# Constants filled inside the encoder program, identity products in TensorE's first waits, and other orders in the last encoder step, the first cross items and the tail

## The reference

```python
# 1: six layers of causal linear attention with MLP, 16 heads of 16, over x flipped along the sequence
for l in range(6):
    a = causal_linear_attn(elu(q) + 1, elu(k) + 1, v) @ Wo[l] + bo[l]
    x = layer_norm(x + a, g1[l], be1[l])
    x = layer_norm(x + gelu(x @ W1[l] + b1[l]) @ W2[l] + b2[l], g2[l], be2[l])
x = layer_norm(x + flip(layer_norm(x)))       # final norm gf, bf, then the residual
# 2: differential cross attention against ctx_1024
attn = softmax(q1 k1 / 4) - gain * softmax(q2 k2 / 4)
x = layer_norm(x + norm_per_head(attn @ v) @ wo.T)
# 3: three cycles of a coupling net
for _ in range(3):
    tf = sigmoid(gelu-net of three layers(out) @ cn_w4 + cn_b4)
    coupling = 0.1 + adaptive_range * (0.7 * gf + 0.3 * tf - 0.5) * 2.0
    out = out + coupling * twist(out)         # twist: (p_r, -p_i, -o_r, o_i)
return layer_norm(x + out)
```

## Time and profile before

| | us |
|---|---|
| median of 3 runs | 1529.33 (1527.33 to 1529.43) |
| profiled execution | 1529.64 |
| its span, first to last instruction | 1527.9 |
| PE busy in the span | 1463.5 |
| DVE, POOL, ACT busy | 1248.2, 1024.9, 984.4 |

### The profile page before, as it was taken

How to read it: one execution, slowest core, us unless ns; L and a number is a source line. 1 busy time by engine, 2 the same in 40 slices (tenths; PEclk the granted TensorE clock), 3 DMA queues, 4 the chain that set the end, 5 groups by cost and what they waited for, 6 DMA issues and landing times. The chain is left out here.

```text
span 1527.9 us, 38603 instructions
## 1 busy us (share of the span) xinstructions
PE 1463.5 (96%) x15935; PEld 1163.1 (76%) x15935; DVE 1248.2 (82%) x2076; ACT 984.4 (64%) x1608; POOL 1024.9 (67%) x970
## 2 busy tenths in 40 slices
PE   6799999999999999999999999999999899999897
PEld 4688888888888888888888888888887566665434
DVE  5888989889898888888888888988784799998546
ACT  4566667666666666667667666666644788887445
POOL 4356667766677566776667766677558599986534
PEclk8899999999999999999999999999999999999999
DMA  5010011110111101210012100110205455443001
GB/s 162 13 60 19 19 26 42 60 24 19 26 46 57 21 19 26 64 42 19 19 26 70 38 17 19 26 43 13 40 9 152 129 165 168 150 154 87 1 0 56
DMA packets 91766, 81.99 MB, mean 54 GB/s; under 512 B 17652, under 2 KB 79816, under 8 KB 91592
## 3 DMA queue, kind: packets, MB, share of 16 engines
q1 hardware_dynamic: 91592, 79.54, 18.3%
HBM read 50.79 MB, written 14.68 MB: 43 GB/s over the span
## 5 line engine op out<-in xcount | busy, mean ns | idle before, releaser
L789 POOL TENSOR_TENSOR e_h_lo<-e_h_f,e_h_hi 128x512 fp32r<-128x512 f32 x192 | 261.7, 1371 | 200.3 <-ACT e_h_hi L581 198.0
L580 ACT ACTIVATE e_h_f<-e_pr,e_h_bias 128x512 f32<-128x512 f32 x192 | 132.0, 688 | 217.9 <-PE e_pr L181 213.3
L900 DVE TENSOR_TENSOR e_am<-e_sc,c_amask 128x1024 f32<-128x1024 f32 x192 | 225.8, 1217 | 51.2 <-PE e_sc L428 51.2
L1900 DVE TENSOR_REDUCE x_mx<-x_psS 128x4 f32<-128x1024 f32 x128 | 154.4, 1210 | 32.1 <-PE x_psS L1484 31.9
L179 PE MATMUL e_tr<-e_W_hi,e_h_hi 128*128 128x256 f32 x576 | 166.1, 288 | 1.1 <-POOL e_h_lo L789 1.1
L179 PE MATMUL e_pr<-e_yT_hi,e_W_hi 128*128 128x512 f32 x384 | 166.8, 434 | 0.3 <-ACT e_h_hi L581 0.3
L180 PE MATMUL e_tr<-e_W_lo,e_h_hi 128*128 128x256 f32 x576 | 163.7, 284 | 0.0
L181 PE MATMUL e_tr<-e_W_hi,e_h_lo 128*128 128x256 f32 x576 | 163.5, 284 | 0.0
L1652 ACT ACTIVATE x_ex<-x_psT 128x1024 f32<-128x1024 f32 x128 | 131.1, 1024 | 43.2 <-PE x_psT L1506 40.5
L180 PE MATMUL e_pr<-e_yT_lo,e_W_hi 128*128 128x512 f32 x384 | 151.6, 395 | 0.0
L181 PE MATMUL e_pr<-e_yT_hi,e_W_lo 128*128 128x512 f32 x384 | 149.8, 390 | 0.0
(11 more groups left out here) (299 smaller groups left out, 4370.2 us busy)
## 6 DMA issues: line engine op xcount, KB each, us to landing
e_raw_m<-in_L_attn_W_dram SPq DMA_DIRECT2D x12, 1024.0 KB, 5.2
x_qs<-query_rows SPq DMA_DIRECT2D x48, 256.0 KB
e_x_raw<-e_x_blocks SPq DMA_DIRECT2D x352, 32.0 KB, 1.9
x_ks<-key_rows SPq DMA_DIRECT2D x48, 128.0 KB, 2.7
query_rows<-x_q_hi SPq DMA_DIRECT2D x16, 256.0 KB, 2.1
query_rows<-x_q_lo SPq DMA_DIRECT2D x16, 256.0 KB, 2.3
x_ctok<-in_ctx_dram SPq DMA_DIRECT2D x8, 256.0 KB, 2.9
x_xo<-in_x_dram SPq DMA_DIRECT2D x8, 256.0 KB, 2.8
```

Source lines behind the costliest of these rows:

```text
L580: act.activation(h_f[:, m % HR, :], ps_pr[m % 2][:, :], ACT.Gelu, bias=h_bias[:, l * FC + m:l * FC + m + 1])
L789: pool.tensor_tensor(h_lo[:, m, :], h_f[:, m % HR, :], h_hi[:, m, :].bitcast(F32), ALU.subtract).then_inc(h_lo_done, 1)
L900: dve.tensor_tensor(am[:, s % 2, c, :, :, :], ps_sc[:, :, c * 2 * P:(c + 1) * 2 * P].rearrange("p r (h n) -> p r h n", n=P), amask[:, :].u ...
L1900: dve.tensor_reduce(mx[:, N % 2, :, 0:HG].rearrange("p i (a h) -> p h a i", a=2)[:, pair], ps_s[pair][:, :, :].rearrange("p a (i j) -> p a ...
```

## The change

GpSimd fills the constants at the head of its encoder program and the separate block is gone; PE waits for the identity alone (semaphore value 2) and multiplies it by itself into free PSUM banks, 11, 8 and 5 times at the start and 8, 14 and 10 times in the step u = 0. The Exp table is asked for at ACT's start. In the last step but one `mlp_up(7)` stands behind the second Wo block and `gelu(7)` behind `attn_hi(1)`. The encoder's last moments and their power move behind the first cross statistics on DVE and POOL, and POOL does `rsqrt(0, 2)` ahead of `keys_lo(1)`. In the tail DVE writes the first tile's couplings and applies half of the last two tiles' norm.

```diff
@@ tensor, step @@
+                def kept_busy(bank, n):
+                    for _ in range(n):
+                        pe.matmul(bank[:, 0:P], ident[:, :], ident[:, :], start=True, stop=True)
+
                 if q < 0:
+                    pe.wait_ge(consts["ready"], consts["unit"])
+                    kept_busy(ps_pr[0], 11)
                     pe.wait_ge(consts["ready"], consts["count"])
                     pe.wait_ge(x0_loaded, 16)
...
+                    kept_busy(ps_pr[0], 8)
                     pe.wait_ge(biases_loaded, 16 * len(BIASES))
...
+                    kept_busy(ps_pr[0], 5)
...
+                if u == 0:
+                    kept_busy(ps_tr[1], 8)
                 if attn:
                     pe.wait_ge(phi_done, 4 * t + 4)
...
+                if u == 0:
+                    kept_busy(ps_tr[1], 14)
                 if attn:
                     pe.wait_ge(ktok_done, t + 1)
...
+                if u == 0:
+                    kept_busy(down_bank(3), 10)
...
                     mlp_up(6)
-                    mlp_up(7)
+                    if following or not attn:
+                        mlp_up(7)
...
+                        elif mlp and s == 2:
+                            mlp_up(7)
                         pe.wait_ge(aT_lo_done, 2 * t + s // 2 + 1)
@@ scalar, step @@
                 if q < 0:
+                    act.wait_ge(consts["ready"], consts["count"])
+                    act.activation(table[:, :], consts["ident"][:, 0:1], ACT.Exp)
...
-                    gelu(7)
+                    if following or not attn:
+                        gelu(7)
...
                     attn_hi(1)
+                if mlp and attn and not following:
+                    gelu(7)
@@ gpsimd @@
             cross = nxt.gpsimd(pool)
+            consts["fill"](pool)
...
-            rsqrt(2, final)
-
...
-            cross.items({N: last_shifted(s) for s, N in enumerate(LAST_SHIFTED)})
+            cross.items({LAST_MOMENTS: lambda: rsqrt(2, final), **{N: last_shifted(s) for s, N in enumerate(LAST_SHIFTED)}})
@@ vector @@
-            moments(2, final)
...
-            cross.items({N: last_rows(half) for half, N in enumerate(LAST_USED)})
+            cross.items({LAST_MOMENTS: lambda: moments(2, final), **{N: last_rows(half) for half, N in enumerate(LAST_USED)}})
@@ cross stage, gpsimd items @@
             x1_norm(1)
+            rsqrt(0, 2)
             keys_lo(1)
-            rsqrt(0, 2)
@@ feed forward @@
+            k, late = j // 2, j % 2
+            if k < PAIRS:
+                sp.wait_ge(y_done, 2 * j + 2)
+            elif late:
+                sp.wait_ge(norm_step, READY * NT + 2 * (k - PAIRS) + 2)
+            else:
+                sp.wait_ge(y_done, SB * PAIRS + 2 * (k - PAIRS) + 2)
             sp.dma_start(ov[:, 2 * j:2 * j + 2], X[:, 2 * j:2 * j + 2]).then_inc(stored, 16)
...
-                    for i in range(PAIRS):
-                        shares(stage, i)
+                    shares(stage, 1)
             for k in range(NT):
-                apply(k)
+                apply(k, SB if k < PAIRS else SB // 2)
...
-            for b in range(2 if stage < HALVES - 1 else 0):
+            for b in range(2 if stage < HALVES - 1 or i == 0 else 0):
...
+        def apply(k):
+            dve.wait_ge(rs_done, 2 * k + 2)
+            for s in range(SB // 2, SB):
+                dve.tensor_scalar(X[:, k * SB + s, :], half_bank(k, s), rs[:, k, s:s + 1], shift[:, k, s:s + 1],
+                                  ALU.mult, ALU.add).then_inc(norm_step, 1)
...
             norm(3)
+            apply(2)
+            apply(3)
```

More of the change, by code:

```diff
@@ L163, in encoder @@
     LNS = {1: 2, 2: 3}
+    LAST_MOMENTS = 0
     LAST_NORMED, LAST_SHIFTED, LAST_USED = (9, 10, 17, 25), (11, 12, 20, 28), (29, 37)
@@ L565, in step @@
                 if attn:
-                    act.activation(table[:, :], consts["ident"][:, 0:1], ACT.Exp)
+                    if q >= 0:
+                        act.activation(table[:, :], consts["ident"][:, 0:1], ACT.Exp)
                     for j in range(2 * KC):
@@ L2119, in sync @@
         for j in range(NB // 2):
-            sp.wait_ge(y_done, 2 * j + 2)
+            k, late = j // 2, j % 2
[5 more added lines that the diff above has]
+                sp.wait_ge(y_done, SB * PAIRS + 2 * (k - PAIRS) + 2)
             sp.dma_start(ov[:, 2 * j:2 * j + 2], X[:, 2 * j:2 * j + 2]).then_inc(stored, 16)
@@ L2285, in fourth, with apply @@
             act.activation(th[:, tile(stage, i), :], banks[L4_BANK[i]][:, :], ACT.Tanh, bias=b4h[:, :], scale=0.5).then_inc(a4, 1)
-        def apply(k):
+        def apply(k, rows):
             act.wait_ge(rs_done, 2 * k + 2)
-            for s in range(SB):
+            for s in range(rows):
                 act.activation(X[:, k * SB + s, :], half_bank(k, s), ACT.Identity, bias=shift[:, k, s:s + 1],
@@ L2298, in shares @@
                 act.activation(cp[:, k, cols], th[:, k, cols], ACT.Identity, bias=offset[:, 2 * k + b:2 * k + b + 1],
-                               scale=slope[:, :]).then_inc(cp_done, 1)
+                               scale=slope[:, :]).then_inc(a4, 1)
         def rows_in(k, bank):
@@ L2465, in shares @@
                                   ALU.mult, ALU.add).then_inc(cp_done, 1)
-            dve.wait_ge(cp_done, 2 * n + 2)
+            if stage < HALVES - 1 or i == 0:
+                dve.wait_ge(cp_done, 2 * n + 2)
+            else:
+                dve.wait_ge(a4, PAIRS * HALVES + 2)
             if stage > 0:
@@ L2525, in constants @@
     blockmask = consts["blockmask"][:, :].rearrange("p (h d) -> p h d", d=HX)
-    with nc.Block() as block:
-        @block.gpsimd
-        def _(pool):
-            pool.memset(ident, 0.0).then_inc(filled, 1)
-            for table in (amask, headmask, consts["blockmask"][:, :]):
-                pool.memset(table, 1.0).then_inc(filled, 1)
-            pool.memset(consts["half"][:, :], -0.5).then_inc(ready, 1)
-            pool.wait_ge(filled, 4)
-            pool.affine_select(ident, ident, [[-1, P]], ALU.not_equal, 1.0, base=0, channel_multiplier=1).then_inc(ready, 1)
-            pool.affine_select(amask, amask, [[-1, P]], ALU.is_ge, 0.0, base=0, channel_multiplier=1).then_inc(ready, 1)
-            pool.affine_select(headmask, headmask, [[-DH, HC]], ALU.is_ge, 0.0, base=0, channel_multiplier=1).then_inc(lower, 1)
-            pool.affine_select(blockmask, blockmask, [[-DH, HC], [0, HX]], ALU.is_ge, 0.0, base=0, channel_multiplier=1).then_inc(lower, 1)
-            pool.wait_ge(lower, 2)
-            pool.affine_select(headmask, headmask, [[DH, HC]], ALU.is_ge, 0.0, base=DH - 1, channel_multiplier=-1).then_inc(ready, 1)
-            pool.affine_select(blockmask, blockmask, [[DH, HC], [0, HX]], ALU.is_ge, 0.0, base=DH - 1, channel_multiplier=-1).then_inc(ready, 1)
@@ L2546, in constants, with fill @@
-    consts["ready"], consts["count"] = ready, 5
+    def fill(pool):
+        pool.memset(ident, 0.0).then_inc(filled, 1)
+        for table in (amask, headmask, consts["blockmask"][:, :]):
+            pool.memset(table, 1.0).then_inc(filled, 1)
+        pool.memset(consts["half"][:, :], -0.5).then_inc(ready, 1)
+        pool.wait_ge(filled, 4)
+        pool.affine_select(ident, ident, [[-1, P]], ALU.not_equal, 1.0, base=0, channel_multiplier=1).then_inc(ready, 1)
+        pool.affine_select(amask, amask, [[-1, P]], ALU.is_ge, 0.0, base=0, channel_multiplier=1).then_inc(ready, 1)
+        pool.affine_select(headmask, headmask, [[-DH, HC]], ALU.is_ge, 0.0, base=0, channel_multiplier=1).then_inc(lower, 1)
+        pool.affine_select(blockmask, blockmask, [[-DH, HC], [0, HX]], ALU.is_ge, 0.0, base=0, channel_multiplier=1).then_inc(lower, 1)
+        pool.wait_ge(lower, 2)
+        pool.affine_select(headmask, headmask, [[DH, HC]], ALU.is_ge, 0.0, base=DH - 1, channel_multiplier=-1).then_inc(ready, 1)
+        pool.affine_select(blockmask, blockmask, [[DH, HC], [0, HX]], ALU.is_ge, 0.0, base=DH - 1, channel_multiplier=-1).then_inc(ready, 1)
@@ L2547, in constants @@
+    consts["ready"], consts["count"], consts["unit"], consts["fill"] = ready, 5, 2, fill
     return consts
```

## The result

The changed kernel takes 1520.11 us (median of 4 runs, 1519.69 to 1521.38) against 1528.84 (4 runs, 1527.33 to 1529.43): the ratio is 0.9949, 95% interval 0.9937 to 0.9961. Its profiled execution took 1520.41 us with a span of 1518.7, 9.2 us less than the span of before. Forecast were 6.4 us less.

What follows compares the result with a forecast made beforehand. It took PE, busy 96% of the span, as the bound. Terms -3.0 - 1.0 - 0.6 - 1.3 - 0.5 = -6.4 from the profiled 1529.64 gave 1523.2 us, range 1519.5 to 1527.5.

Steps and rivals of the forecast that it cites:

- The block: At the start: without the constants block SP issues its first load at about 0.79, 2.72 us sooner; `X` there at 5.0.
- The start's products: At the start: products take back nearly all the block gives, clock rises at 6.6, queries at 11.15; start's term -3.0 us.
- 27.8 to 37.3: 0: Low-clock stretch from 27.8 to 37.3 us, without products: should fall to 1.2 GHz again, so 0 gained.
- The rival that the clock stays up there: Rival: the clock also stays up from 27.8 to 37.3, some 2.5 us more, 1520.7 us; chance 0.12.
- u = 0: 1.0: Step u = 0: products 0.2 us late, but full clock saves 1.2; term -1.0 us, between 0 and -1.3.
- Last step but one: 0.6: Last encoder step but one: moved `mlp_up(7)` fills PE's 1.83 us wait, POOL limits the gain; -0.6 us, 0 to -1.4.
- First items: 1.3: First cross items: reordering removes PE waits of 0.64 and 0.71 us; term -1.3 us, between 0 and -2.0.
- Tail: 0.5: Kernel end: ACT and DVE share the norm, so the last transfer issues sooner; -0.5 us, between -0.2 and -0.9.
- Late engines: Rival at the start: the other engines don't leave the first meeting at 0.79; 1524.1 us, chance 0.09.
- Constants held back by DVE's clearing: Rival at the start: the identity comes 2.1 us later, start's term -0.9; 1525.3 us, chance 0.08.
- Late rise and nothing at the borders: Rival: late clock rise at the start, POOL's queue and SP's order take back the steps' gain; 1527.3 us, chance 0.14.
- Products that don't raise the clock: Rival at the start and u = 0: identity products leave the clock at 1.2 GHz; +6.0 us, 1535.6 us, chance 0.05.

Runs made afterwards that it cites:

- e1: The changed kernel without its 24 identity products at the start; 1520.96 us.
- e6: The kernel before with only the constants moved into GpSimd's encoder program and the early Exp table; 1526.31 us, ratio 0.9981.
- b2: The changed kernel with 6, 3 and 0 identity products at the start, and 5, 8 and 10 added in the first step's waits; 1516.52 us.
- e5: The changed kernel run again, unchanged; 1520.36 us.

## Why the prediction was right in range and short in size

- **The block** (SP at 0.79, `X` at 5.0). Right: 0.79 in every trace, `X` at 4.56 and 4.96 where nothing stood ahead of it (e1, e6), instead of 7.73, and e6 alone gives 2.4 us by 22.67 and 3.1 in the median, against 2.72.
- **The start's products.** The forecast let the clock rise at 6.6, within 5.85 to 7.25; the two traces of the program have 7.9 and 5.2, and gains of 3.09 and 4.41 us, the latter beyond the term's bound of 3.4. "The products take back nearly all that the missing block gives" is right. That the queries began at 11.13, against 11.15, is in part luck: the clock rose 1.3 us later than taken, and the products were shorter (0.44 and 0.22 us against 0.45 and 0.24). What the sum lacked is that the clock without them is as loose: it rose 3.7 us after the first query in e1, 5.4 after it before and 5.8 in e6.
- **27.8 to 37.3: 0.** This term failed, 1.30 us in the first trace. "Should fall to 1.2 GHz again" was right, that it would last as long was not: 10.2 us in six of the ten traces without products in that step, 6.8 in four, with one program on both sides. And what it takes differs less from trace to trace than its length, since a short one followed a late start (3.09 and 1.30) and a long one an early start (4.41 and 0.25). The rival that the clock stays up there did not come: it fell in both traces of the changed kernel. Only b2 and its successors, with products there, kept it up.
- **u = 0: 1.0.** The clock was 1.00 throughout, and from `mlp_up(0)` to the second scores came 1.09 us by the clock against 1.17. The 0.2 us of delay was a gain of 0.2 us. 1.29 in the trace, at the upper bound of 0 to 1.3.
- **Last step but one: 0.6.** 1.4 us earlier at Wo, right to 0.1 us, and PE's wait ahead of the transposes grew from 0.55 to 1.61, as said. `x_ve` did not shrink (1.36 to 1.34); only POOL's wait of 1.59 ahead of it went, by 0.3. Measured 0.34.
- **1171: 0.** No step names this place, and the sum put it at nothing. Some 1.5 us, over half of the whole miss of 2.8, are here, by a fall of the clock that the kernel before had in its profiled execution and the changed one in neither. The trace of before showed it, and the forecast took none of its low stretches as that execution's own.
- **First items: 1.3.** Measured 0.80. 0.85 came at `x_x` and 1.02 by `x_psT`, of which 0.64 and 0.71 are the waits and the rest mostly the clock. Then 0.78 went back in the wait for the load behind the keys' store, and 0.3 further on. The store was issued 0.75 us later against PE's work, near the 0.5 forecast, but "hidden while these are a batch ahead" failed.
- **Tail: 0.5.** 0.5, by luck: 0.3 of it come from the couplings, put at 0, and the divided norm, put at 0.5, gives 0.16, since the sum followed the last transfer to its issue and not to its end.
- **Rivals.** Late engines: SP at 0.79. Constants held back by DVE's clearing: 0.29 us beside it, as alone. Late rise and nothing at the borders: the clock rose by 7.9, and steps and items gave 1.1 us. The Trainium skill's rule in SBUF — State Buffer, section "SBUF: two separate sides", would have had 2.1 us more if the clearing is an operation of that mode; the trace shows none. Products that don't raise the clock: all eight transposes of e5 are at 2.4 GHz, with nothing but products ahead.
- **The range.** It held in part by luck. The best bounds of the terms add up to -9.0 (the text has -8.9), 1520.6; the traces' gain is 9.2 and the median 1520.11, beyond all of them together. The measurement is inside only because the range, from 1519.5, was drawn wider than its working, and the surplus came from places that the working had at 0. Besides, 1523.2 counts from the profiled execution, 1529.64; from the median it would be 1522.9.

## What to carry to other kernels

Fill a wait of TensorE with products only up to its length: nine that fit at the start made the kernel 2.6 us faster than the 24 that did not. Where another engine ends last, as in u = 0, ten more cost nothing. Before a term is put on a low-clock stretch, see whether the same program shows it in a second trace, for its begin and length move by microseconds between executions. And where an order changes on one engine, look at what the queue engine then issues ahead of small loads: one store in the wrong place cost 1.1 us. Follow a transfer to its end and not only to its issue: the last store went out 0.5 us sooner and the kernel ended 0.16 sooner.

## What the runs showed of the hardware

The granted clock fell at 1171 in one execution and not in another with the same work ahead (5.85 and 5.92 of 7.00 us busy); the low time in the first step was 6.8 us in one execution of the changed kernel and 10.2 in the next. DVE's clearing of 1.76 us ran beside GpSimd's six selects on the constants, which took 0.29, 0.29, 0.20, 0.40, 0.19 and 0.37 us, against 0.29, 0.29, 0.19, 0.39, 0.19 and 0.37 alone before. Two output transfers issued 0.41 us apart at the end had the span end 3.25 to 3.27 us behind the second, in 11 traces; 0.91 us apart it was 2.93 to 3.00, in three.
